# Attention stage of a four-stage kernel: the maximum is subtracted before the turn, and the exponential is taken after it, with host-made key blocks of 64 rows

## What is computed

```python
x = x + tanh(g_xattn[0]) * L0_xattn(ctx, ctx, layernorm(x), ssm_kernel, D)   # gated long convolution
x = x + tanh(g_ffn[0])   * L0_ffn(layernorm(x), ...)                          # 8 experts, top 2, and a shared one
x = x + tanh(g_xattn[1]) * L1_xattn(layernorm(x), ctx, ctx)                   # the stage of this change
x = x + tanh(g_ffn[1])   * L1_ffn(layernorm(x), ...)                          # 32 experts, top 6, and a shared one
```

```python
scores = einsum("bhqd,bhkd->bhqk", q, k) * 16 ** -0.5
scores = where(k_index > q_index, -inf, scores)
out    = softmax(scores) @ v
```

## Time and profile before

| | us |
|---|---|
| median of 3 runs | 1000.56 |
| lowest, highest | 995.88, 1001.1 |
| the profiled execution | 996.23 |
| its span on the core | 994.4 |
| mean granted clock of PE | 0.982 |

### The profile page before, as it was taken

How to read it: one execution, slowest core, us unless ns; L and a number is a source line. 1 busy time by engine, 2 the same in 40 slices (tenths; PEclk the granted TensorE clock), 3 DMA queues, 4 the chain that set the end, 5 groups by cost and what they waited for, 6 DMA issues and landing times. The chain is left out here.

```text
span 994.4 us, 14954 instructions
## 1 busy us (share of the span) xinstructions
PE 938.3 (94%) x4768; PEld 737.1 (74%) x4784; DVE 608.4 (61%) x1441; ACT 522.2 (53%) x1274; POOL 156.3 (16%) x113
## 2 busy tenths in 40 slices
PE   6899889999999999799999877999999999999997
PEld 6799767877888888655555555787778888888886
DVE  6678654465645555477777763565865555555554
ACT  3222143433543333277677553666766676666665
POOL 5899200000000000163444100000000000000000
PEclk9899999999999999899999898999999999999999
DMA  9100210323211321210000113444444434444443
GB/s 307 39 1 2 67 61 17 120 81 107 70 49 49 104 77 53 57 57 17 11 16 16 37 33 101 127 145 130 140 128 144 126 114 147 133 152 134 149 127 117
DMA packets 50271, 88.54 MB, mean 89 GB/s; under 512 B 6528, under 2 KB 15360, under 8 KB 49824
## 3 DMA queue, kind: packets, MB, share of 16 engines
q1 hardware_dynamic: 49488, 87.61, 28.8%
q10 hardware_dynamic: 720, 0.14, 0.1%
HBM read 85.31 MB, written 2.42 MB: 88 GB/s over the span
## 5 line engine op out<-in xcount | busy, mean ns | idle before, releaser
L734 DVE TENSOR_TENSOR ylof<-yf,yhif 128x512 fp32r<-128x512 f32 x200 | 138.1, 691 | 176.1 <-ACT yhif L647 175.7
L877 PE MATMUL bank<-xhf,whif 128*128 128x512 f32 x528 | 212.2, 402 | 1.5 <-ACT rf L622 1.5
L877 PE MATMUL bank<-xlf,whif 128*128 128x512 f32 x528 | 208.7, 395 | 0.0
L877 PE MATMUL bank<-xhf,wlof 128*128 128x512 f32 x528 | 208.7, 395 | 0.0
L647 ACT ACTIVATE yhif<-yf 128x512 fp32r<-128x512 f32 x200 | 125.6, 628 | 89.5 <-DVE yf L747 82.8
L906 PE MATMUL bank<-yhif,whif 128*128 128x512 f32 x400 | 159.9, 400 | 12.8 <-DVE ylof L734 12.7
L906 PE MATMUL bank<-yhif,wlof 128*128 128x512 f32 x400 | 158.0, 395 | 0.0
L906 PE MATMUL bank<-ylof,whif 128*128 128x512 f32 x400 | 157.1, 393 | 0.0
L624 ACT ACTIVATE rf<-bank 128x512 f32<-128x512 f32 x136 | 81.1, 596 | 124.9 <-PE bank L877 124.1
L877 PEld LDWEIGHTS bank<-xhf,whif 128*128 128x128 f32 x528 | 99.5, 189 | 24.6 <-ACT rf L622 1.9
L877 PEld LDWEIGHTS bank<-xhf,wlof 128*128 128x128 f32 x528 | 99.7, 189 | 24.0
(11 more groups left out here) (126 smaller groups left out, 1179.0 us busy)
## 6 DMA issues: line engine op xcount, KB each, us to landing
Gf<-gates SPq DMA_DIRECT2D x160, 256.0 KB, 3.7
wrawf<-in_wu SPq DMA_DIRECT2D x68, 256.0 KB, 2.7
wrawf<-in_wu SPq DMA_DIRECT2D x32, 384.0 KB, 3.1
ctx_windows<-in_ctx_win SPq DMA_DIRECT2D x3, 1024.0 KB, 11.8
toeplitz<-in_kpad SPq DMA_DIRECT2D x4, 512.0 KB, 9.2
X<-in_x SPq DMA_DIRECT2D x4, 512.0 KB, 9.2
v_slot<-in_ctx_nat SPq DMA_DIRECT2D x16, 128.0 KB, 2.1
out_y<-X SPq DMA_DIRECT2D x8, 256.0 KB, 2.8
```

The lines of the kernel that those rows point to most:

```text
L734: dve.tensor_tensor(ylo[:, K % S, :], y[:, K % S, :], yhi[:, K % S, :].bitcast(F32), ALU.subtract).then_inc(s_yl, 1)
L877: last = pe.matmul(o, w_[:, Nu % S, wc], x_[:, c, xs], start=(m == 0), stop=(m == 5))
```

## The change

The whole attention stage is rewritten; the rest of the kernel only lends it two arrays and some semaphores.

- Keys: the host makes, for every batch and quad, a block of 64 rows by 512 columns: the 64 columns of ctx that belong to the four heads, turned, with head h's 16 rows filled in its 128 columns and zero elsewhere. The score matmul contracts over these 64 rows. The blocks (128 KB each, 64 of them) are loaded one by one into six slots. `KT`, the mask and POOL's products go.
- Queries: four transposes, each turning 64 columns into 64 partitions, and one copy on ACT that also carries the scale.
- Normalization of the rows moves from DVE to ACT, with the shift (minus mean times deviation) made by POOL for half of the batches at a time.
- Softmax: DVE takes the maxima (not negated) and subtracts them (`shifted`, 512 columns, PSUM to SBUF); PE turns the differences (`turned`); ACT takes one exponential of 512 columns from PSUM to SBUF (`probs`). The copy `pt_copy` and the collected sums go.
- Values: the host pads each head's 16 columns to 32, of which the 17th is one, so that the value matmul also gives the sums (256 KB a batch, two slots). `inverse` reads them from the bank that `out_rows` fills.
- Order: quads are numbered through (n = 4b + t). Scores are three banks deep: PE issues the scores of quad n + 2, turns quad n, multiplies the values of quad n - 1. All loops are written out.

In the diff a removed function that has stood above is left out with "...", and the indentation is cut.

```diff
+def negated(dve, phase, part):
+    bs = part_of(phase, part)
+    dve.tensor_scalar(nmean[:, bs], mv[:, bs, 0], -1.0, None, ALU.mult).then_inc(shift_sems[phase][0], 1)
+def shifts(pool, phase, part):
+    bs = part_of(phase, part)
+    pool.wait_ge(shift_sems[phase][0], part + 1)
+    pool.wait_ge(deviation_sems[phase][2], part + 1)
+    pool.tensor_tensor(nshift[:, bs], nmean[:, bs], rstd[:, bs], ALU.mult).then_inc(shift_sems[phase][1], 1)
...
-    KT = sb("ctx_nat_t_sb", [P, 2, T], ctx=pc)
-    headmask = sb("headmask", [P, 8], ctx=pc)
+    KLR, SR, DR, PR = 6, 3, 3, 3
+    NQ = 4 * NB
     causal = sb("causal", [P, 4, P], BF16, pc)
     identb = sb("identb", [P, P], BF16, pc)
-    KP = sb("k_heads", [P, 2, 2, 8, P], ctx=pc)
-    V = sb("v_slot", [P, 2, D + HD1], ctx=pc)
+    KM = sb("k_blocks_sb", [64, KLR, 4 * P], ctx=pc)
+    V = sb("v_slot", [P, 2, NH1, 32], ctx=pc)
     xn = sb("xn_c", [P, 2, D], ctx=pc)
-    qT = sb("q_t", [P, 2, 2, P], ctx=pc)
-    nmax = sb("neg_max", [P, 2, NH1], ctx=pc)
-    Pr = sb("probs", [P, 8, P], ctx=pc)
-    den = sb("den", [P, 2, NH1], ctx=pc)
-    rden = sb("rden", [P, 2, NH1], ctx=pc)
-    PT = sb("probs_t", [P, 2, 4, P], ctx=pc)
+    Q1 = sb("q_t", [64, 2, 4, P], ctx=pc)
+    nmax = sb("max", [P, DR, 4], ctx=pc)
+    Ds = sb("shifted_scores", [P, DR, 4, P], ctx=pc)
+    PT = sb("probs_t", [P, PR, 4 * P], ctx=pc)
     oT = sb("o_t", [P, 4, P], ctx=pc)
+    rden = sb("rden", [P, NH1], ctx=pc)
     ov = sb("o_norm", [P, D], ctx=pc)
...
+    s_sh = shift_sems["c"][1]
+    s_kl = s_cq + s_cg[0:2]
+    s_vl = [s_cg[2], s_kt[0]]
+    LOADED = 16
...
+    def s_bank(n):
+        return bk(n % SR)
+    x_bank, o_bank, row_bank = bk(3), bk(6), bk(7)
+    def turn_bank(n):
+        return bk(4 + n % 2)
     with nc.Block() as block:
         @block.sync
         def _(sp):
...
+            def keys(n):
+                if n >= KLR:
+                    sp.wait_ge(s_s, n - KLR + 1)
+                sp.dma_start(KM[:, n % KLR, :], k_blk[n]).then_inc(s_kl[n % KLR], 16)
+            def vals(b):
+                if b >= 2:
+                    sp.wait_ge(s_pv, 4 * (b - 2) + 4)
+                sp.dma_start(V[:, b % 2].rearrange("p h d -> p (h d)"), v_rows[b]).then_inc(s_vl[b % 2], 16)
+            keys(0)
+            keys(1)
+            sp.dma_start(causal[:], causal_c).then_inc(s_cc, 16)
+            sp.dma_start(identb[:], identb_c).then_inc(s_cc, 16)
+            for n in range(2, KLR):
+                keys(n)
+            vals(0)
+            vals(1)
+            for n in range(KLR, NQ):
+                keys(n)
+                if n % 4 == 0 and n // 4 + 1 < NB and n // 4 >= 2:
+                    vals(n // 4)
+            vals(NB - 1)
         @block.gpsimd
         def _(pool):
...
             deviations(pool, "c", 1)
...
+            shifts(pool, "c", 1)
             deviations(pool, "f1", 0)
         @block.tensor
         def _(pe):
...
+            def queries(b):
                 pe.wait_ge(s_n, b + 1)
...
+                if b > 0:
+                    pe.wait_ge(s_qt, b)
+                for t in range(4):
+                    last = pe.transpose(x_bank[0:64, t * P:(t + 1) * P], xn[:, b % 2, 64 * t:64 * t + 64], ident[:])
                 last.then_inc(s_xt, 1)
...
+            def scores(n):
+                b, t = n // 4, n % 4
+                if n >= SR:
+                    pe.wait_ge(s_d, n - SR + 1)
+                pe.matmul(s_bank(n), identb[:], causal[:].rearrange("p h k -> p (h k)"), start=True, stop=False)
+                pe.wait_ge(s_kl[n % KLR], LOADED + 16 * (n // KLR + 1))
                 if t == 0:
...
                     pe.wait_ge(s_qt, b + 1)
...
+                pe.matmul(s_bank(n), Q1[:, b % 2, t, :], KM[:, n % KLR, :], start=False, stop=True).then_inc(s_s, 1)
+            def turned(n):
+                pe.wait_ge(s_d, n + 1)
+                if n >= 2:
+                    pe.wait_ge(s_e, n - 1)
+                for g in range(4):
+                    last = pe.transpose(turn_bank(n)[:, g * P:(g + 1) * P], Ds[:, n % DR, g, :], ident[:])
+                last.then_inc(s_tt, 1)
+            def values(n):
+                b, t = n // 4, n % 4
+                pe.wait_ge(s_e, n + 1)
                 if t == 0:
...
+                    pe.wait_ge(s_vl[b % 2], LOADED + 16 * (b // 2 + 1))
+                    if b > 0:
+                        pe.wait_ge(s_oe, b)
                 for g in range(4):
...
+                    last = pe.matmul(o_bank[32 * g:32 * g + 32, t * P:(t + 1) * P], V[:, b % 2, 4 * t + g, :],
+                                     PT[:, n % PR, g * P:(g + 1) * P], start=True, stop=True, skip_group_check=True)
                 last.then_inc(s_pv, 1)
...
+            def out_rows(b):
+                pe.wait_ge(s_oe, b + 1)
+                if b > 0:
+                    pe.wait_ge(s_sc, b)
                 for t in range(4):
...
+                    last = pe.transpose(row_bank[:, t * P:(t + 1) * P], oT[:, t, :], ident[:])
                 last.then_inc(s_ot, 1)
...
+            keep_clock(pe, bk(0), 20)
+            queries(0)
             pe.wait_ge(s_cc, 32)
...
+            scores(0)
+            scores(1)
+            for n in range(NQ):
+                b, t = n // 4, n % 4
+                if n + 2 < NQ:
+                    scores(n + 2)
+                turned(n)
+                if n > 0:
+                    values(n - 1)
+                if t == 0 and b + 1 < NB:
+                    queries(b + 1)
+                if t == 2 and b > 0:
+                    out_rows(b - 1)
+            values(NQ - 1)
+            out_rows(NB - 1)
         @block.scalar
         def _(act):
...
+            def normed(b):
+                act.wait_ge(s_sh, b // (2 * BPB) + 1)
+                if b >= 2:
+                    act.wait_ge(s_xt, b - 1)
+                act.activation(xn[:, b % 2, :], X[:, b, :], ACT.Identity, bias=nshift[:, b:b + 1],
+                               scale=rstd[:, b:b + 1]).then_inc(s_n, 1)
+            def q_copy(b):
+                act.wait_ge(s_xt, b + 1)
+                if b >= 2:
+                    act.wait_ge(s_s, 4 * (b - 1))
+                act.activation(Q1[:, b % 2].rearrange("p t q -> p (t q)"), x_bank[0:64, :], ACT.Copy, scale=SCALE1).then_inc(s_qt, 1)
+            def probs(n):
+                act.wait_ge(s_tt, n + 1)
+                if n >= PR:
+                    act.wait_ge(s_pv, n - PR + 1)
+                act.activation(PT[:, n % PR, :], turn_bank(n), ACT.Exp).then_inc(s_e, 1)
             def out_copy(b):
...
+                act.wait_ge(s_pv, 4 * b + 4)
+                if b > 0:
+                    act.wait_ge(s_ot, b)
+                act.activation(oT[:].rearrange("p t q -> p (t q)"), o_bank, ACT.Copy).then_inc(s_oe, 1)
+            normed(0)
+            normed(1)
+            q_copy(0)
+            for n in range(NQ):
+                b, t = n // 4, n % 4
+                if t == 1 and b + 1 < NB:
+                    q_copy(b + 1)
+                if t == 1 and b > 0:
+                    out_copy(b - 1)
+                probs(n)
+                if t == 2 and b + 2 < NB:
+                    normed(b + 2)
             out_copy(NB - 1)
         @block.vector
         def _(dve):
...
+            def maxima(n):
+                dve.wait_ge(s_s, n + 1)
+                dve.tensor_reduce(nmax[:, n % DR, :], s_bank(n).rearrange("p (h k) -> p h k", k=P), AX_X, ALU.max).then_inc(s_m, 1)
+            def shifted(n):
+                dve.wait_ge(s_m, n + 1)
+                if n >= DR:
+                    dve.wait_ge(s_tt, n - DR + 1)
+                dve.tensor_tensor(Ds[:, n % DR], s_bank(n).rearrange("p (h k) -> p h k", k=P),
+                                  nmax[:, n % DR, :].unsqueeze(2).broadcast_to((P, 4, P)), ALU.subtract).then_inc(s_d, 1)
+            def inverse(b):
+                dve.wait_ge(s_ot, b + 1)
+                dve.reciprocal(rden[:], row_bank.rearrange("p (h d) -> p h d", d=32)[:, :, HD1]).then_inc(s_rc, 1)
+            def scaled(b):
+                dve.wait_ge(s_rc, b + 1)
+                dve.tensor_tensor(ov[:].rearrange("p (h d) -> p h d", d=HD1),
+                                  row_bank.rearrange("p (h d) -> p h d", d=32)[:, :, 0:HD1],
+                                  rden[:].unsqueeze(2).broadcast_to((P, NH1, HD1)), ALU.mult).then_inc(s_sc, 1)
+            def residual(b):
+                dve.wait_ge(s_sc, b + 1)
+                dve.scalar_tensor_tensor(X[:, b, :], ov[:], tg[:, 1:2], X[:, b, :], ALU.mult, ALU.add).then_inc(s_xd, 1)
+            def moments(b):
+                dve.wait_ge(s_xd, b + 1)
+                dve.bn_stats(stats[:, b, :], X[:, b, :]).then_inc(s_sd, 1)
+            maxima(0)
+            shifted(0)
             variances(dve, "c", 1)
...
+            negated(dve, "c", 1)
+            for n in range(NQ):
+                b, t = n // 4, n % 4
+                if n + 1 < NQ:
+                    maxima(n + 1)
```

(62 more changed lines are left out.)

225 lines of the change are left out of this document (24 added, 201 removed).

## The result

| | before | after |
|---|---|---|
| median of 4 runs, us | 998.22 | 1016.51 |
| lowest, highest | 995.68, 1001.1 | 1014.7, 1022.39 |
| the profiled execution, its span | 996.23, 994.4 | 1014.7, 1012.9 |

The ratio is 1.0206, with a 95% interval of 1.0177 to 1.0235. Forecast were 1013 us and a range of 997 to 1026.

The account below looks back on a forecast made before the run. PE was taken to bound the attention stage. -5.6 + 3.3 + 16.0 + 0.9 = +14.6 gave 1010.8 us from the profiled execution, 1015.2 from the median; the forecast between them was 1013 us, range 997 to 1026.

Parts of the forecast that it names:

- The softmax, -5.6: Attention stage: with softmax moved behind the turn, PE's waits for exps go, 5.6 us less.
- The queries, +3.3: Query transposes: four of 64 columns instead of two of 128, 0.22 us a batch for 15 batches, +3.3 us.
- The shape, +16.0: Score matmul: 64 round trips between full-size and 64-row pieces at 0.25 us each, +16.0, between 8.3 and 28.8.
- The start, +0.9: Start of the attention stage: first scores wait for four query transposes and ACT's query copy, +0.9 us.
- the loads, 0: Loads of keys and values on SP's queue: they land within the 5.0 us PE has, cost 0.
- The sum behind it, +14.6: Whole kernel: -5.6 + 3.3 + 16.0 + 0.9 = +14.6 us on the profiled execution's 996.23.
- The rival "64 rows cost no more than 128": Score matmul: no price for 64 rows, sum -1.4, thus 995 to 999 us; chance 0.26.
- The rival of half-time passes: Score matmul: a 64-row pass runs in half the time, 972 to 977 us; chance 0.09 with other faster ways.

Follow-up runs that it names:

- 96-row kernel: The changed kernel with 32 rows of zeros below the 64 of every key block and of the queries: 998.41 us beside 998.45 before, ratio 0.9995.
- the doubled one: The changed kernel with every quad's score matmul done twice over 64 rows into the same bank at half the scale: 1071.64 us, one execution.

## Why the prediction was right

**The direction and its cause** were right. PE's own work bounded the stage, so nothing that was taken off ACT, DVE and POOL could give more than PE's waits, and what was added to PE showed in full.

**The softmax, -5.6.** Right in size, in part by luck. The starts give 5.2 us of waits. Of the rows that were added up, the 2.2 in front of the scores were missing records of the causal matmul, and the 3.4 in front of the causal matmul were too low, since the real delay is 0.35 a batch. The prediction's own numbers had the hint: 0.29 + 0.16 is more than the 0.33 that were left over in a batch. The waits are gone in the profile after. The 96-row kernel stands level with before, and the one without the extra query transposes is 2 us ahead.

**The queries, +3.3.** Right in size: the stage takes 151.8 with four transposes (96 rows) and 148.7 with two. By the medians it is 998.41 beside 998.45 before, and 994.41 beside 996.53, so some 2 to 4 us. Their 64 columns cost no change of shape: from the first of them to the causal matmul it takes 488.56 - 488.10 = 0.46, four times 0.11 and a few hundredths.

**The shape, +16.0.** The mechanism held, the size was off: this is the term that was mis-sized. The step was a round trip of 0.25, taken between bounds of 0.13 and 0.45. Measured are 0.34 a quad and 21.4 over the stage. I had seen from the values only that the next matmul started 0.10 late and set the way back at the same 0.10. On the way into 64 rows the first pass starts 0.09 late and then another 0.10 is lost within it, and on the way out some 0.05 for a weight load comes on top of the 0.10. The router's small transposes, whose bounds do hold 0.34, deserved more weight than the values. The values' own round trip was 0.24, too, and not 0.20.

**The start, +0.9, and the loads, 0.** The stage's first scores come 423.14 - 415.60 = 7.5 us after its first matmul, against 6.8 before: +0.8. The loads never made PE wait in the changed kernel.

**The sum.** With what was measured it is -5.2 + 3.3 + 21.4 + 0.8 = +20.3; the stage itself grew by 21.5, the spans by 18.5, the medians by 18.3. The forecast of 1013 was 3.5 low and lay inside its range. The sum behind it, +14.6, was 7 low for the stage; in the profiled execution 3 of these came back outside the stage, over 2 of them by the clock, which nothing in the prediction had foreseen. So that the number came this near is in part luck. A term was left out as well: the output rows' transposes now stand behind the values and take 478.00 - 477.51 = 0.49 (96 rows) instead of 0.43, some 0.9 over the stage. Between 430 and 560 us PE was busy 98% of the time, as forecast, ACT 39% and DVE 65%, below the 45% and 75% expected; neither was a limit. The rival "64 rows cost no more than 128" is what the 96-row kernel looks like, and it gave 998.4, within the 995 to 999 that stood for it. The rival of half-time passes is excluded: a pass of 512 columns takes 0.43 over 64, 96 and 128 rows alike.

The rule of the Trainium skill (TensorEngine Tiling (Array Packing), Key Properties) that changing the tiling mode drains TensorE agrees with these runs, now for 64 rows too, with 0.19 us on the way in and 0.16 on the way out. The same page's speedup of up to 2x (Theoretical Speedup) for contractions of at most 64 did not appear with one 64-row piece at work at a time; no run here had two side by side.

## What to carry to other kernels

Where PE bounds a stage, look at the sequence of shapes that it is given, not only at columns: a matmul over 64 rows between full-size ones cost some 0.34 us here, as much as 400 columns of an fp32 pass, and padding it with zero rows to 96 or 128 took that away. If narrow pieces are needed, put them next to each other; the 32-column pieces ran four at a time, which by the estimate above saved more than the 0.24 of their way in and back. And before work is taken off an engine, read how long the bounding engine waits for it: 5 us was all there was to win from ACT, however busy it looked. Read such waits from distances between starts, since a missing record looks like a wait.

## What was not expected of the hardware

- The price is a step, not a slope: 64 rows cost some 0.34 us a round trip, 96 rows nothing to the hundredth.
- Half of the way in hides inside a record: the first pass lasts 0.69 instead of 0.59. Distances between starts of single kernels put it down to the pass; the doubled one (0.96, then 0.95) shows it to be the change.
- From the first value pass to 64-row passes behind them is 0.36 us, just what it is to a full-size matmul: with one change fewer a quad was 0.10 us shorter.
- PE's clock at the start of the following stage differs between the two profiled executions (0.62 and 1.00 granted in the first 7 us). It moved the span by over 2 us, more than some of the terms of the sum.
